# Rows of a tile in the order (chunk, step): new layouts for x, the parked rows and the states, and half the semaphore clears on ScalarE

## The chip, the cores and the metric

The kernel runs on one core of one Trainium2 chip. The metric is device time in microseconds (us) of one launch, the median of several runs.

## The reference, cut to what matters

Two blocks, each adding to x (8 batches, 1024 steps, 256 features, float32). The modulation vectors sa, ca, ga, sb, cb, gb come from a small matrix product with the condition vectors; ga and gb are kept away from zero.

```python
h = layernorm(x) * (1 + ca) + sa
# block 1: a recurrence over the 1024 steps of each batch
hs[t] = tanh(hs[t-1] @ A.T + h[:, t] @ B.T);  y[t] = hs[t] @ C.T
x = x + ga * (layernorm(y + h) * gamma + beta)
h = layernorm(x) * (1 + cb) + sb
# block 2: a recurrence over the 8 batches, each step on all 1024 rows
f = sigmoid(h[b] @ wf.T + c @ uf.T + bf); i = ...; g = tanh(...)
c = f * c + i * g
# after the last batch
x = x + gb * tanh(h @ wo.T + c_final @ uo.T + bo)
```

The scan of block 2 runs over the first axis, so its state c has one row for each position of the sequence. The kernel runs this scan for four blocks of positions, one after the other.

## The kernel before, in words

**Chunks.** Each batch is cut into K = 16 chunks of L = 64 steps. All 8 x 16 = 128 chunks are stepped together, so one step of block 1 is four products of 128 columns (two halves H of the features in, two out; the trace shows each as two PE instructions, since they are float32), and a state is 128 features x 128 chunks, twice. A first run over steps 18 to 63 of every chunk gives the state that the next chunk starts from; a check at the end (`again`) would repeat everything if a chunk's end state had moved since. In the profiled run there is one pass.

**Phase one** (`unit1`, to about 137 us) takes pairs of steps: SyncE (`SP`) loads 128 x 512 of x, VectorE (`DVE`), ScalarE (`ACT`) and GpSimd (`POOL`) normalise it, SP writes the normalised rows to a scratch tensor in HBM, `h_park` (L493), TensorE (`PE`) transposes them (L1425) and multiplies by B (L1408). Beside it the recurrence of the warm-up steps runs (`recur1`, L1373, then `summed`, L1448), with `tanhs`, `starts` and `summed` of ACT writing the states `hs` (L763, L768, L825).

**Phase two** (`unit2`) is a software pipeline, one tile after the other. There are 32 tiles; one is 256 rows, those of one batch and 16 steps of all its 16 chunks, in two halves j of 8 steps. The order on each engine is that of the calls in its own `unit2`. A unit holds: two steps of the recurrence (PE `step` L1462, DVE L1108 or L1111, ACT L832 or L835); `high` on ACT (L842) and `low` on POOL (L653, in phase one on DVE, L1095), which split the float32 states of a pair of steps into a rounded part `hsh` and a rest `hsl`; `project` (L1489), the product of these with C; the loads of the parked rows (`load_h`, L511) and of x (`load_x`, L518); normalisation, the three gates (L1503), the product with wo (L1557); and the store of a finished tile (`store`, L553), two DMAs of 128 x 256. Four states are held in `hs` (step t in slot t % 4), 8 steps in each half of `hsh` and `hsl`.

**The order of rows.** A tile's 128 partitions are in the order (step, chunk): 8 steps, and 16 chunks in each. `x_t`, `h_park_t` and `out_t` are the views that give this order for the three kinds of DMA.

**The end.** After the last unit, `last_outputs` on each engine finishes seven tiles that wait for the final c, and then the last tile in two halves (DVE L1283, POOL L728). SP reads the flag `again`, clears the first 25 of the 50 semaphores of `of_middle`, issues 14 stores in the order of `STORES` and the last two (L611), clears the other 25, waits until the four compute engines are through (`r_over`), clears the 20 of `of_end`, waits for all stores to land (`s_out`) and ends the round. `walk` and `rounds` only repeat the units.

Of the kernel before, what the change touches and what calls it, by code (L numbers as in the profile page):

```python
# [20 lines left out]
def adaln_kernel(nc, x, A, B, C, gamma, beta, wf, uf, bf, wi, ui, bi, wc, uc, bc, wo, uo, bo, in_c, cond, wmod, out):  # L21
# [71 lines left out]
    with ctx:  # L93
# [277 lines left out]
        def pair_of(t, first):  # L371

            return t[:, :, :, first:first + 2, :].rearrange("p m b t k -> p m b (t k)")

        def by_chunk(t):
            return t.rearrange("p (b k) -> p b k", b=NB)

        def by_half(t):
            return t.rearrange("p (m b k) -> p m b k", m=H, b=NB)
# [34 lines left out]
        def split_of(n, few, state_of):  # L414

            if n < NU - 2:
                return few[:, n % 2, :, :]
            i = (n - NU + 2) * H * POS
            return state_of[:, 0].rearrange("p m b t k -> p (m b t k)")[:, i:i + H * POS].rearrange("p (k n) -> p k n", k=H)
# [33 lines left out]
        def _(sp):  # L453
# [31 lines left out]
            def unit1(v, ref):  # L485
# [20 lines left out]
            def load_h(c):  # L506
# [3 lines left out]
                for i in range(2):  # L510
                    sp.dma_start(hin[:, c % 3, i * D:(i + 1) * D],  # L511
                                 h_park_t[b + i, T * TB + j * HT:T * TB + (j + 1) * HT, :, :]).then_inc(s_h[c % 3], 16)
# [32 lines left out]
            def store(o):  # L545
# [6 lines left out]
                for j in range(2):  # L552
                    sp.dma_start(out_t[o % NB, steps(o, j), :, :],  # L553
# [33 lines left out]
            with sp.Fori(0, left) as r:  # L587
# [17 lines left out]
                half = len(of_middle) // 2  # L605
                clear(of_middle[0:half])
                for o in STORES:
                    store(o)
                for j, done, n in ((0, s_fin, LAST + len(ON_DVE) + 1), (1, s_fp, len(ON_POOL) + 1)):
                    sp.wait_ge(done, n)  # L610
                    sp.dma_start(out_t[(NU - 1) % NB, steps(NU - 1, j), :, :], tiles_of(NU - 1)[:, j, :]).then_inc(s_out, 16)  # L611
                clear(of_middle[half:])
# [9 lines left out]
        def _(pool):  # L622
# [25 lines left out]
            def low(p):  # L648
# [4 lines left out]
                pool.tensor_tensor(pair_of(hsl[:, j], t), pair_of(hs, 2 * p % 4), pair_of(hsh[:, j], t).bitcast(f32),  # L653
# [1056 lines left out]
```

## Time and profile before

| what | value |
|---|---|
| median of 3 runs | 567.81 us (567.32 to 568.59) |
| the profiled execution's own time | 568.92 us |
| its span, first to last instruction | 567.0 us |
| PE busy | 546.8 us (96%) |
| DVE, ACT, POOL busy | 381.7, 341.6, 342.3 us |
| granted PE clock | 0.994 of full speed (2.4 GHz) |
| DMA | 64.09 MB in 58,513 packets, 49,736 of them under 2 KB |

PE is matrix multiplication; its weight loads (PEld) overlap it. Busy times of different engines lie beside each other, so a time counts towards the end only where the others wait for it. "Chain" is the line of work followed back from the last instruction, each piece to what released it. DMA instructions stand under SPq, the queue of SyncE that issues them; semaphore clears do not appear in the rows and show as gaps.

### The profile page before, as it was taken

The page shows a single profiled execution, that of the slowest core. Times are in us where ns is not written, and L with a number is a line of the kernel's source. Part 1 is how long each engine was busy: PE and PEld are TensorE (multiplying, and loading weights), DVE is VectorE, ACT ScalarE, POOL GpSimd, SP SyncE. Part 2 cuts the span into 40 slices and gives each one's busy share as a digit, 9 for nine tenths or more (in the row PEclk, how much of TensorE's full clock was granted, in tenths as well). Part 3 has the DMA queues.
Part 4 walks back from the last instruction along what each step waited for, and adds up shares of the span by engine and source line. Part 5 has one row for each costly group of instructions (what it writes and reads, how often), then busy time and mean ns, then how long its engine had stood idle before and what let it go on. Part 6 is the DMA issues. An engine that isn't in the chain of part 4 may idle for free.

```text
span 567.0 us, 13418 instructions
## 1 busy us (share of the span) xinstructions
PE 546.8 (96%) x4616; PEld 534.8 (94%) x4616; DVE 381.7 (67%) x908; ACT 341.6 (60%) x862; POOL 342.3 (60%) x475
## 2 busy tenths in 40 slices
PE   6999999999989999999999999999999999999992
PEld 3899999999879999999999999999999999999992
DVE  5888888885757665555766566666566677666763
ACT  3777777775466555465656565666655557567550
POOL 4677777660475444454766666677666667677353
PEclk9999999999999999999999999999999999999997
DMA  8556445435243222222233333333233343242354
GB/s 278 154 191 199 150 149 150 135 96 156 89 129 110 66 65 69 78 70 76 58 103 102 103 103 93 115 109 119 94 94 94 94 127 115 76 117 71 82 96 149
DMA packets 58513, 64.09 MB, mean 113 GB/s; under 512 B 5408, under 2 KB 49736, under 8 KB 58448
## 3 DMA queue, kind: packets, MB, share of 16 engines
q1 hardware_dynamic: 58448, 63.26, 37.1%
q8 instruction: 36, 0.59, 0.4%
q14 instruction: 29, 0.24, 0.1%
HBM read 46.44 MB, written 16.81 MB: 112 GB/s over the span
## 4 chain that ended last, share of the span: by engine, by line
PE 90%; DVE 3%; ACT 2%; POOL 2%; issue 1%; DMA 1%; SPq 0%; POOLq 0%; DVEq 0%; ACTq 0%
PE psOF L1503 14%; PE psI L1503 14%; PE psG L1503 13%; PE psWR L1557 7%; PE psWR L1462 7%; PE psWR L1408 4%; PE psOF L1408 4%; PE psWR L1373 4%; PE psC L1489 4%; PE psOF L1489 3%; PE psOF L1373 3%; PE psT L1536 2%; PE psT L1425 1%; PE psWR L1448 1%; PE psOF L1448 1%
## 5 line engine op out<-in xcount | busy, mean ns | idle before, releaser
L646 POOL TENSOR_TENSOR hin<-hin,uvec 128x256 f32<-128x256 f32 x64 | 51.0, 817 | 32.5 <-ACT hin L808 31.6
L653 POOL TENSOR_TENSOR hsl<-hs,hsh 128x512 fp32r<-128x512 f32 x24 | 30.9, 1288 | 51.5 <-DVE state L1215 31.6
L928 ACT ACTIVATE psOF<-psOF,biasT 128x256 f32<-128x256 f32 x64 | 26.0, 444 | 57.8 <-PE psOF L1503 57.8
L1203 DVE SCALAR_TENSOR_TENSOR lo<-psT,cb1T,hi 128x256 fp32r<-128x256 f32 x60 | 26.3, 480 | 46.5 <-ACT hi L873 46.5
L1111 DVE TENSOR_TENSOR pre<-psWR,state 128x256 f32<-128x256 f32 x44 | 18.6, 424 | 48.6 <-PE psWR L1462 48.6
L1462 PE MATMUL psWR<-hs,AT 128*128 128x128 f32 x368 | 49.6, 275 | 1.5 <-ACT hs L835 0.8
L660 POOL TENSOR_TENSOR xin<-xin,tA 128x512 f32<-128x512 f32 x32 | 41.5, 1298 | 12.7 <-DMA tA<-rows_d 12.7
L687 POOL TENSOR_TENSOR zn<-zn,tA 128x512 f32<-128x512 f32 x32 | 41.3, 1292 | 12.4 <-ACT zn L846 12.4
L846 ACT ACTIVATE zn<-state,nmA,rstdA 128x256 f32<-128x256 f32 x64 | 35.0, 594 | 20.3 <-POOL nmA L677 20.3
L1462 PEld LDWEIGHTS psWR<-hs,AT 128*128 128x128 f32 x368 | 45.3, 191 | 1.9 <-ACT hs L835 1.0
L1065 DVE SCALAR_TENSOR_TENSOR hin<-xin,mvA,uvec 128x256 f32<-128x256 f32 x56 | 40.3, 759 | 9.8 <-DMA h_park<-hin 9.4
L682 POOL TENSOR_TENSOR wx<-wx,tG 128x512 f32<-128x512 f32 x24 | 36.5, 1519 | 11.2 <-ACT wx L894 11.1
L700 POOL TENSOR_TENSOR wx<-wx,uvec 128x512 f32<-128x512 f32 x24 | 31.1, 1295 | 14.6 <-DVE state L1215 12.5
L846 ACT ACTIVATE xn<-state,nmB,rstdB 128x256 f32<-128x256 f32 x64 | 34.8, 590 | 5.6 <-POOL nmB L709 5.6
L928 ACT ACTIVATE gg<-psG,biasT 128x256 f32<-128x256 f32 x64 | 27.0, 475 | 16.6 <-PE psG L1503 16.6
L835 ACT ACTIVATE hs<-pre 128x256 f32<-128x256 f32 x44 | 18.4, 417 | 30.4 <-DVE pre L1111 30.2
L1503 PE MATMUL psOF<-hi,wfT_hi 128*128 128x256 f32 x120 | 33.6, 280 | 2.4 <-DVE gf L1223 2.4
L1503 PE MATMUL psI<-hi,wiT_hi 128*128 128x256 f32 x120 | 35.9, 299 | 0.0
L928 ACT ACTIVATE psI<-psI,biasT 128x256 f32<-128x256 f32 x64 | 26.0, 446 | 14.9 <-PE psI L1503 14.9
L808 ACT ACTIVATE hin<-hin,rstdA 128x256 f32<-128x256 f32 x64 | 28.7, 497 | 9.6 <-POOL rstdA L639 9.6
L1503 PE MATMUL psOF<-lo,wfT_hi 128*128 128x256 f32 x120 | 33.3, 278 | 0.0
L1503 PE MATMUL psI<-lo,wiT_hi 128*128 128x256 f32 x120 | 33.3, 278 | 0.0
(351 smaller groups left out, 2306.5 us busy)
## 6 DMA issues: line engine op xcount, KB each, us to landing
h_park<-hin SPq DMA_DIRECT2D x32, 256.0 KB, 2.2
hin<-h_park SPq DMA_DIRECT2D x64, 128.0 KB
xin<-in_L_attn_x_dram SPq DMA_DIRECT2D x64, 128.0 KB
tA<-rows_d SPq DMA_DIRECT2D x32, 256.0 KB, 4.4
out_dram<-state SPq DMA_DIRECT2D x64, 128.0 KB
xin<-in_L_attn_x_dram SPq DMA_DIRECT2D x28, 256.0 KB, 2.9
tW<-rows_d SPq DMA_DIRECT2D x32, 128.0 KB, 3.9
tG<-rows_d SPq DMA_DIRECT2D x24, 128.0 KB, 4.1
```

Source lines behind the costliest of these rows:

```text
L646: pool.tensor_tensor(h, h, sa, ALU.add).then_inc(a_h, 1)
L660: pool.tensor_tensor(xg, xg, both(tA[:, m % 2, D:W]), ALU.add).then_inc(s_xg, 1)
L687: pool.tensor_tensor(two(zn[:, :]), two(zn[:, :]), both(tA[:, m % 2, 0:D]), ALU.mult).then_inc(s_zg, 1)
L846: act.activation(dst[:, j * D:(j + 1) * D], tiles_of(m)[:, j, :], ACT.Identity, bias=nm[:, j:j + 1], scale=rstd[:, j:j + 1]).then_inc(done, 1)
L928: act.activation(dst[:, m_ * POS:(m_ + 1) * POS], src[:, m_ * POS:(m_ + 1) * POS], fn, bias=biasT[:, i, m_, n % NB:n % NB + 1]).then_inc(s, 1)
L1065: dve.scalar_tensor_tensor(halfw(dst, tt), halfw(src, tt), mv[:, tt, 0:1], ca1, ALU.subtract, ALU.mult).then_inc(a_tmp, 1)
L1373: ins = pe.matmul(sums1(v.c - R1LAG)[m][:, tt * P:(tt + 1) * P], AT[:, k, m * P:(m + 1) * P], hs[:, k, :, 1 - tt, :], start=False, stop=(k ...
L1408: last = pe.matmul(ps, w["B"][:, k, m * P:(m + 1) * P], h[:, (ref - back) % 2, k * 2 * P:(k + 1) * 2 * P], start=(n % (3 * H) == 0), stop= ...
L1462: ins = pe.matmul(ps, AT[:, k, m * P:(m + 1) * P], hs[:, k, :, (t - 1) % 4, :], start=(k == 0 and (separate or m == 0)), stop=(k == H - 1 ...
L1489: last = pe.matmul(ps[:, i * D:(i + 1) * D], h[:, j, k, b + i, :, :].rearrange("p t k -> p (t k)"), w["C"][:, k, :], start=(n == 1 and i = ...
L1503: last = pe.matmul(ps[:, at + m * columns:at + (m + 1) * columns], w[name][:, k, m * P:(m + 1) * P], xx[:, k, :], start=(start and n == 1) ...
L1557: last = pe.matmul(ps[:, j * D:(j + 1) * D], h[:, k, j * P:(j + 1) * P], w["wo"][:, k, :], start=(n < HELD and c == 1 and j == 0), stop=(c ...
```

## The change: what it does

1. DRAM side: rows of a tile go in the order (chunk, step); `x_t`, `out_t` are rearranged, `h_park` is laid out as [chunk row, step, feature], like x.
2. `hs` becomes [slot, half, chunk row], so a state is one contiguous run. `hsh` and `hsl` get the step as innermost axis: for one chunk row its 8 steps lie side by side. So `high` and `low` now read `hs` in runs of 128 and read or write `hsh`, `hsl` at a stride of 8 elements (32 bytes), where before all runs had 32 elements.
3. The clears of the first half of `of_middle` move from SP, where they stood ahead of the stores, to the end of ACT.

```diff
-    x_t = x.rearrange("b (k t) d -> b t k d", k=K)
-    out_t = out.rearrange("b (k t) d -> b t k d", k=K)
+    x_t = x.rearrange("b (k t) d -> b k t d", k=K)
+    out_t = out.rearrange("b (k t) d -> b k t d", k=K)
-    h_park = nc.dram_tensor("h_park", [L, P, D], f32, kind="Internal").ap()
-    h_park_t = h_park.rearrange("t (b k) d -> b t k d", b=NB)
+    h_park = nc.dram_tensor("h_park", [P, L, D], f32, kind="Internal").ap()
...
-        hsh = sb("hsh", [P, 2, H, NB, HT, K], f32r)
-        hsl = sb("hsl", [P, 2, H, NB, HT, K], f32r)
-        hs = sb("hs", [P, H, NB, 4, K])
+        hsh = sb("hsh", [P, 2, H, P, HT], f32r)
+        hsl = sb("hsl", [P, 2, H, P, HT], f32r)
+        hs = sb("hs", [P, 4, H, P])
...
         def pair_of(t, first):
-            return t[:, :, :, first:first + 2, :].rearrange("p m b t k -> p m b (t k)")
+            return t[:, :, :, first:first + 2].rearrange("p m n t -> p m t n")
+
+        def two_of(first):
+            return hs[:, first:first + 2, :, :].rearrange("p t m n -> p m t n")
+
+        def step_of(t):
+            return hs[:, t, :, :].rearrange("p m n -> p (m n)")
...
-                    sp.dma_start(h_park[bass.ds(p * 2, 2), :, :].rearrange("t p d -> p t d"),
+                    sp.dma_start(h_park[:, bass.ds(p * 2, 2), :],
                                  two(htok(ref - 2)))...
...
                     sp.dma_start(hin[:, c % 3, i * D:(i + 1) * D],
-                                 h_park_t[b + i, T * TB + j * HT:T * TB + (j + 1) * HT, :, :])...
+                                 h_park[(b + i) * K:(b + i + 1) * K, T * TB + j * HT:T * TB + (j + 1) * HT, :])...
...
-                                 x_t[m % NB, steps(m, j), :, :]).then_inc(s_x[m % 2], 16)
+                                 x_t[m % NB, :, steps(m, j), :]).then_inc(s_x[m % 2], 16)
...
-                    sp.dma_start(out_t[o % NB, steps(o, j), :, :],
+                    sp.dma_start(out_t[o % NB, :, steps(o, j), :],
...
                 sp.wait_ge(s_Ul, 2)
-                half = len(of_middle) // 2
-                clear(of_middle[0:half])
                 for o in STORES:
                     store(o)
...
-                clear(of_middle[half:])
+                clear(of_middle[len(of_middle) // 2:])
...
-                pool.tensor_tensor(pair_of(hsl[:, j], t), pair_of(hs, 2 * p % 4), pair_of(hsh[:, j], t).bitcast(f32),
+                pool.tensor_tensor(pair_of(hsl[:, j], t), two_of(2 * p % 4), pair_of(hsh[:, j], t).bitcast(f32),
                                    ALU.subtract).then_inc(s_hsl, 1)
...
-                    act.activation(hs[:, :, :, t % 4, :], by_half(pre[:, :]), ACT.Tanh).then_inc(s_tanh, H)
+                    act.activation(step_of(t % 4), pre[:, :], ACT.Tanh).then_inc(s_tanh, H)
...
-                act.activation(pair_of(hsh[:, j], t), pair_of(hs, 2 * p % 4), ACT.Copy).then_inc(s_hsh, 1)
+                act.activation(pair_of(hsh[:, j], t), two_of(2 * p % 4), ACT.Copy).then_inc(s_hsh, 1)
...
                 act.activation(psR[:, 0:D], psR[:, 0:D], ACT.Tanh).then_inc(s_ot, 1)
+                act.wait_ge(s_fin, LAST + 1)
+                for s in of_middle[0:len(of_middle) // 2]:
+                    act.sem_clear(s)
...
                         ins = pe.matmul(sums1(v.c - R1LAG)[m][:, tt * P:(tt + 1) * P], AT[:, k, m * P:(m + 1) * P],
-                                        hs[:, k, :, 1 - tt, :], start=False, stop=(k == H - 1), skip_group_check=True)
+                                        hs[:, 1 - tt, k, :], start=False, stop=(k == H - 1), skip_group_check=True)
...
-                            last = pe.matmul(ps[:, i * D:(i + 1) * D], h[:, j, k, b + i, :, :].rearrange("p t k -> p (t k)"), w["C"][:, k, :],
+                            last = pe.matmul(ps[:, i * D:(i + 1) * D], h[:, j, k, (b + i) * K:(b + i + 1) * K, :].rearrange("p k t -> p (k t)"), w["C"][:, k, :],
```

The other edits write the same forms at the other places that touch `hs` (the tanhs of phase one, `starts`, the copies `h_end` and `h_skip`, the check at the end, the products L1448 and L1462).

## Rows read from the trace of the kernel before

**Rows 1.** Busy us (instructions) of PE, PEld, DVE, ACT, POOL; PEclk; DMA share; GB/s.

```profile
0.00:17.00 17.00, 11.96 (x33) 5.62 (x34) 10.88 (x32) 6.17 (x13) 8.35 (x23) 1.00 0.78 263
137.00:170.00 33.00, 29.77 (x254) 27.68 (x252) 22.19 (x67) 15.79 (x43) 17.37 (x26) 1.00 0.40 123
170.00:444.00 274.00, 273.96 (x2367) 273.57 (x2367) 173.48 (x411) 160.54 (x390) 165.24 (x217) 1.00 0.30 90
```

**Rows 2.** State products and transposes (L1536): ns min/median/max, first and last start.

```profile
L1462 PE MATMUL psWR<-hs,AT x368: 270/275/377, 142.8 to 435.8; 128*128 128x128 f32 x184
...
L1536 PE MATMUL psT<-ident,xn x128: 270/272/328, 153.4 to 530.0; 128*128 128x128 f32 x128
```

**Rows 3.** Groups by shape: high, low, two state copies: us busy, mean ns.

```profile
L653 POOL TENSOR_TENSOR hsl<-hs,hsh 128x512 fp32r<-128x512 f32 x24 | 30.9, 1288 | 51.5 <-DVE state L1215 31.6 <-DVE state L1147 19.9
...
L842 ACT ACTIVATE hsh<-hs 128x512 fp32r<-128x512 f32 x32 | 20.1, 628 | 0.3
...
L1095 DVE TENSOR_TENSOR hsl<-hs,hsh 128x512 fp32r<-128x512 f32 x8 | 5.5, 682 | 1.7 <-ACT hsh L842 1.7
...
L1191 DVE COPY h_skip<-hs 128x256 f32<-128x256 f32 x1 | 0.6, 640 | 0.0
...
L1101 DVE COPY h_end<-hs 128x256 f32<-128x256 f32 x1 | 0.3, 294 | 0.1
```

**Rows 4.** ACT in phase one: start us, us, instruction, idle before it.

```profile
115.50 0.67 ACT L825 ACTIVATE hs<-psOF 128x128 f32<-128x128 f32 x2 [0.72 <-PE psOF L1448]
```

**Rows 5.** ACT and POOL at the start of phase two, in order of time.

```profile
153.24 0.61 ACT L842 ACTIVATE hsh<-hs 128x512 fp32r<-128x512 f32 x1
...
154.14 1.27 POOL L653 TENSOR_TENSOR hsl<-hs,hsh 128x512 fp32r<-128x512 f32 x1
155.37 0.24 POOL L677 TENSOR_TENSOR nmA<-ngA,rstdA 128x2 f32<-128x2 f32 x1
```

**Rows 6.** The chain in the same stretch: start us, us, what.

```profile
156.03 1.10 ACT zn L846 x2
...
159.30 1.28 POOL hsl L653
...
170.04 1.60 PE psOF L1503 x12
```

**Rows 7.** Waits over the span: waiting instruction, releaser: us, times, longest.

```profile
ACT psOF L928 <- PE psOF L1503: 57.8, 28, 2.9
...
POOL nmB L709 <- ACT ngB L862: 36.0, 25, 2.8
...
SPq L500 <- DMA out_dram<-state: 0.6, 1, 0.6
```

**Rows 8.** DMA instructions on SP by line: ns min/median/max.

```profile
L493 SPq DMA_DIRECT2D h_park<-hin x32: 373/384/410, 11.0 to 126.5; - x32
...
L553 SPq DMA_DIRECT2D out_dram<-state x62: 593/642/707, 282.2 to 561.2; - x62
```

**Rows 9.** SP about its clears and at the end: start us, us.

```profile
282.19 1.34 SPq L553 DMA_DIRECT2D out_dram<-state  x2
287.90 0.67 SPq L511 DMA_DIRECT2D hin<-h_park  x1
...
548.08 1.25 SPq L553 DMA_DIRECT2D out_dram<-state  x2
...
552.56 1.37 SPq L553 DMA_DIRECT2D out_dram<-state  x2
...
561.95 1.34 SPq L611 DMA_DIRECT2D out_dram<-state  x2
```

**Rows 10.** The first and the last of the results stored at the end.

```profile
550.53 0.69 DVE L1278 TENSOR_TENSOR state<-psI,state 128x512 f32<-128x512 f32 x1
...
558.05 0.72 POOL L728 TENSOR_TENSOR state<-wx,state 128x256 f32<-128x256 f32 x1
```

**Rows 11.** A window after the last computation, columns as in rows 1.

```profile
561.00:566.00 5.00, 0.00 (x0) 0.00 (x0) 0.00 (x0) 0.00 (x0) 0.00 (x0) 0.50 0.53 186
```

More of the change, by code:

```diff
@@ L418, in split_of @@
             i = (n - NU + 2) * H * POS
-            return state_of[:, 0].rearrange("p m b t k -> p (m b t k)")[:, i:i + H * POS].rearrange("p (k n) -> p k n", k=H)
+            return state_of[:, 0].rearrange("p m n t -> p (m n t)")[:, i:i + H * POS].rearrange("p (k n) -> p k n", k=H)
         def hi_at(n):
@@ L610, in _ @@
                     sp.wait_ge(done, n)
-                    sp.dma_start(out_t[(NU - 1) % NB, steps(NU - 1, j), :, :], tiles_of(NU - 1)[:, j, :]).then_inc(s_out, 16)
-                clear(of_middle[half:])
+                    sp.dma_start(out_t[(NU - 1) % NB, :, steps(NU - 1, j), :], tiles_of(NU - 1)[:, j, :]).then_inc(s_out, 16)
+                clear(of_middle[len(of_middle) // 2:])
                 sp.wait_ge(r_over, r * 4 + 4)
@@ L762, in tanhs @@
                     act.wait_ge(a_r, v.lin(4, -4 * R1LAG + 2 * tt + m + 1))
-                    act.activation(hs[:, m, :, tt, :], by_chunk(sums1(v.c - R1LAG)[m][:, tt * P:(tt + 1) * P]), ACT.Tanh).then_inc(a_tanh, 1)
+                    act.activation(hs[:, tt, m, :], sums1(v.c - R1LAG)[m][:, tt * P:(tt + 1) * P], ACT.Tanh).then_inc(a_tanh, 1)
             def starts():
                 for m in range(H):
-                    act.activation(hs[:, m, :, 3, 1:K], by_chunk(sums1(RP1 - 1)[m][:, P:2 * P])[:, :, 0:K - 1], ACT.Tanh).then_inc(a_start, 1)
+                    act.activation(by_chunk(hs[:, 3, m, :])[:, :, 1:K], by_chunk(sums1(RP1 - 1)[m][:, P:2 * P])[:, :, 0:K - 1], ACT.Tanh).then_inc(a_start, 1)
             def unit1(v, ref):
@@ L824, in summed @@
                     act.wait_ge(s_r, 2 * t + m + 1)
-                    act.activation(hs[:, m, :, t % 4, :], by_chunk(sums1(RP1 + t // 2)[m][:, t % 2 * P:(t % 2 + 1) * P]), ACT.Tanh).then_inc(s_tanh, 1)
+                    act.activation(hs[:, t % 4, m, :], sums1(RP1 + t // 2)[m][:, t % 2 * P:(t % 2 + 1) * P], ACT.Tanh).then_inc(s_tanh, 1)
             def step(t):
@@ L831, in step @@
                         act.wait_ge(s_pre, n_pre(t) + m + 1)
-                        act.activation(hs[:, m, :, t % 4, :], by_chunk(pre[:, m * P:(m + 1) * P]), ACT.Tanh).then_inc(s_tanh, 1)
+                        act.activation(hs[:, t % 4, m, :], pre[:, m * P:(m + 1) * P], ACT.Tanh).then_inc(s_tanh, 1)
                 else:
                     act.wait_ge(s_pre, n_pre(t) + 2)
-                    act.activation(hs[:, :, :, t % 4, :], by_half(pre[:, :]), ACT.Tanh).then_inc(s_tanh, H)
+                    act.activation(step_of(t % 4), pre[:, :], ACT.Tanh).then_inc(s_tanh, H)
             def high(p):
@@ L1094, in low @@
                 j, t = p // 4 % 2, p % 4 * 2
-                dve.tensor_tensor(pair_of(hsl[:, j], t), pair_of(hs, 2 * p % 4), pair_of(hsh[:, j], t).bitcast(f32),
+                dve.tensor_tensor(pair_of(hsl[:, j], t), two_of(2 * p % 4), pair_of(hsh[:, j], t).bitcast(f32),
                                   ALU.subtract).then_inc(s_hsl, 1)
@@ L1100, in boundary @@
                 dve.wait_ge(a_tanh, 4 * RP1)
-                dve.tensor_copy(by_half(h_end[:, :]), hs[:, :, :, 1, :]).then_inc(a_end, 1)
+                dve.tensor_copy(h_end[:, :], step_of(1)).then_inc(a_end, 1)
             def step(t):
@@ L1190, in unit2 @@
                     dve.wait_ge(s_tanh, 4 * SP0)
-                    dve.tensor_copy(by_half(h_skip[:, :]), hs[:, :, :, (SKIP - 1) % 4, :]).then_inc(s_skip, 1)
+                    dve.tensor_copy(h_skip[:, :], step_of((SKIP - 1) % 4)).then_inc(s_skip, 1)
                 if u == ML:
@@ L1238, in unit2 @@
                     dve.wait_ge(s_hsl, PAIRS)
-                    dve.tensor_tensor(by_half(pre[:, :]), hs[:, :, :, (L - 1) % 4, :], by_half(h_end[:, :]), ALU.subtract).then_inc(k_diff, 1)
+                    dve.tensor_tensor(pre[:, :], step_of((L - 1) % 4), h_end[:, :], ALU.subtract).then_inc(k_diff, 1)
                     dve.wait_ge(k_diff, 1)
-                    near = hs[:, 0, 0:4, :, :].rearrange("p b t k -> p (b t k)")
+                    near = step_of(0)
                     dve.tensor_scalar(near, pre[:, :], -TOL, None, ALU.is_ge).then_inc(k_diff, 1)
@@ L1286, in body @@
                 prepare()
-                dve.tensor_copy(hs[:, :, :, 1, :], by_half(h_skip[:, :])).then_inc(a_end, 1)
-                dve.memset(hs[:, :, :, 3, 0:1], 0.0).then_inc(a_end, 1)
+                dve.tensor_copy(step_of(1), h_skip[:, :]).then_inc(a_end, 1)
+                dve.memset(by_chunk(step_of(3))[:, :, 0:1], 0.0).then_inc(a_end, 1)
                 walk(dve, RUNS1, unit1)
@@ L1448, in summed @@
                         ins = pe.matmul(sums1(RP1 + t // 2)[m][:, t % 2 * P:(t % 2 + 1) * P], AT[:, k, m * P:(m + 1) * P],
-                                        hs[:, k, :, (t - 1) % 4, :], start=False, stop=(k == H - 1), skip_group_check=True)
+                                        hs[:, (t - 1) % 4, k, :], start=False, stop=(k == H - 1), skip_group_check=True)
                     ins.then_inc(s_r, 1)
```

8 lines of the change are left out of this document (3 added, 5 removed).

## Prediction

> **What bounds the kernel now.** I read the page's busy shares, then the busy time by stretches, then PE's waits, and then the end of the span alone. PE is busy 96% of the span and holds 90% of the chain. From 170 to 444 us it is busy 273.96 of 274.00 us [rows 1]: the reader is to see that nothing a feeding engine gains there can count, and that it loses nothing either while its slack lasts. Three places differ. One is the length of PE's own instructions. The second is the start of phase two, 137 to 170 us, where PE is idle 3.2 us [rows 1] and the chain leaves it for POOL, ACT and DVE until 170.04 [rows 6]. The third is the end: the last result is done at 558.05 + 0.72 = 558.77 us [rows 10], the span ends at 567.0, and all 8.2 us between belong to SP and the stores. Of the profiled execution's 568.92 us, 1.9 lie outside the span. It ran 1.11 us above the median of the runs, 567.81; I make the sum on the profile and take the difference off the median.
>
> **The stores at the end.** SP issues 16 DMAs from 552.56 to 561.95 + 1.34 = 563.29 us, 0.671 us each [rows 9]. They form a queue with no gap: the last result is 3.2 us old when its store begins. While they drain and no engine computes, the DMA share is 0.53 at 186 GB/s, 8.5 of 16 engines [rows 11]. So the pattern (8 steps outside, 16 chunks inside) uses eight engines, and these are full. Loads with 128 rows outside reach 0.78, 12.5 engines, in the first 17 us [rows 1]; after the change 16 chunks are outside, and I assume that more than eight work, up to 16. At 16 x 128 KB = 2.1 MB and 186 GB/s the stores need 11.3 us; issue alone needs nearly the same 10.7.
> The Trainium skill, DMA: Bandwidth & Descriptors, "Why a DMA increments its semaphore by 16 and not by 1", says that the number of engines is the largest up to 16 that divides the outermost dimension on both sides: 8 before, 16 after the change. The trace agrees (8.5 engines here).
>
> The clears: 69 of them stood between 282.19 + 1.34 and 287.90 us, 4.37 us, so 0.063 us each [rows 9]. Before the 16 stores SP is free at 549.33 and starts at 552.56 [rows 9]; this gap holds the flag's load and 25 clears (1.6 us). The first result was ready at 550.53 + 0.69 = 551.22 [rows 10]. Without the clears the load ends at about 552.56 - 1.6 = 551.0, so the first store starts at 551.27: 1.3 us earlier. On ACT the 25 clears come after its last tanh, beside DVE's and POOL's last work and the stores; they cost nothing unless ACT ends later than SP's queue, which leaves them some 3 us.
>
> How long one issue takes is the first open number. A tile's store takes 0.593 to 0.707 us, 0.642 at the median; the store of parked rows, with 256 runs of 1 KB instead of 128, only 0.384 [rows 8]. So the count of runs does not set it; either the eight engines or the different shapes of the two sides do. Only the first goes away. Bounds: 0.384 + 0.05 between issues = 0.43 us, and 0.65 (0.593 + 0.05, with the queue less loaded). I take 0.65, the instruction's own row, since the shapes still differ. Then issues end at 551.27 + 16 x 0.65 = 561.7 instead of 563.3. Behind the last issue SP has 45 clears, 2.84 us, and before it waited another 0.6 for the last landing [rows 7]. With the engines half loaded a store lands beside the clears, so the end follows 3.1 instead of 3.7 us after the issues: 564.8 us, **2.2 us less**. At 0.43 us the queue follows the results instead: the last two issues start at 558.4 and 558.85, end at 559.3, and the span ends at 562.4, 4.6 less.
>
> **PE.** The products with the states read 128 columns in 8 runs of 16; they take 275 ns at the median, a transpose that reads 128 columns in one run 272 [rows 2]. Six groups (L1373, L1448, L1462) hold 880 such instructions, the largest of them is shown. At 3 ns each that is 2.6 us; if the runs are not the reason it is 0. The 48 between 137 and 170 us, where PE waits anyway, don't count. I take **2.0 us less**, a little under the row, since the medians are whole ns.
>
> **High and low.** Before: ACT 628 ns, DVE 682, POOL 1288 [rows 3]. After, each element written goes 32 bytes on, and so do those read from `hsh`. No row shows such an access. Lower bound: no loss, since runs of 16 and 32 elements cost none. Upper bound: the slowest copy of a state took 640 ns where the same shape took 294 [rows 3] (POOL was in `low` beside it), a factor of 2.2, so 1370, 1490 and 2810 ns. I take 1.5, in the middle: 0.31 us more on ACT, 0.34 on DVE, 0.64 on POOL.
> The Trainium skill bears on this twice. Vector Engine (DVE) Microarchitecture Reference, "Measured stream behaviour on trn2", has full rate only for runs of two adjacent words and 2.5 instead of 1.05 ns a column for a step of 24 words; GPSIMD Engine Reference, "Performance pitfalls for Q7 kernels", has half as much again for reads with a step over 8 bytes. No row here shows either. The second gives my value for POOL; the first would be a factor of 2.4, and its sum is the rival below.
>
> Where it counts: in full flow not at all. ACT waits 2.1 us a unit for PE ahead of the first gate, which comes after `high`, and POOL waits 1.4 us a unit for ngB, which comes after `low` [rows 7]. In phase one ACT has 0.72 us idle a unit [rows 4], so `high` may grow by that. At the start of phase two it does count. ACT's `high` (153.24) precedes the mean that POOL needs for nmA (155.37), POOL's `low` (154.14) stands right before it [rows 5], and the next `low` (159.30) is itself a piece of the chain that ends with PE's restart at 170.04 [rows 6]. With ACT longer by d and POOL by p the restart is later by d + 2p less about 0.3 of slack (ACT began the normalisation behind it at 156.03 [rows 6], nmA was there at 155.61). 0.31 + 1.28 - 0.3 = **1.3 us more**; the ends are 0 and 0.74 + 3.04 - 0.3 = 3.5. If the cover in full flow were gone, each of 22 units would add the excess.
>
> **The rest.** Parked rows are written as 128 runs of 2 KB instead of 256 of 1 KB, tile loads spread over more engines: no chain piece waits for them, cost 0. Tanhs write one run instead of 8 or 16: below 0.03 us each, on engines with slack, 0. The copies and the check: single instructions, 0.
>
> **Sum.** -2.2 - 2.0 + 1.3 = -2.9 us: profile 566.0, median **564.9 us**.
>
> **Rivals.**
> A: the eight engines were what made an issue slow. For it: rows with sixteen engines are at 0.384. Against: those have equal shapes on both sides. 2.4 us more gain: 562.5. Chance 0.22.
> B, the other side: the strided access is expensive. It acts at the three pieces at 153, 154 and 159 us, and from a factor of 2.1 also on ACT in phase one, where the idle 0.72 is used up and PE waits in each of about four units. With factor f the price is 3.2(f - 1) - 0.3; it outweighs the 4.2 us of gains from f = 2.4, and with phase one from 2.3. At f = 3: 6.1 at the restart, 4 x 0.5 in phase one, less 4.2: 571.7. For it: one access per line of memory everywhere in `high` and `low`. Against: these engines already take 2.5 ns (POOL) and 1.2 ns (ACT) an element, which may cover it. Chance 0.13. At the skill's factor of 2.4 on all three the sum would be about 568.3, the mildest form of B.
> C: the 3 ns on PE have another cause (a product is not a transpose) and stay: 566.9, within the noise. Chance 0.15; a store that still uses eight engines would look the same in the total, with the queue as full as before.
> Forecast: 0.50, with its own range 563.4 to 566.3.
>
> **How the numbers follow.** Best of all bounds: -4.6 - 2.6 = 560.6. Worst short of B: -2.2 + 3.5 = 569.1. The range for 8 in 10 goes from 562.2, just under A, through the forecast and C to 567.8, leaving most of B and the coincidence of all gains outside. This kernel's runs tell 0.2% (1.1 us) from no change. Faster: the forecast and A, 0.72; same: C, 0.15; slower: B, 0.13.
>
> **What would show it.** Stores: the DMA share at the end no longer flat at 0.53, the first store 0.1 us behind its result instead of 1.3, the last issue to the end about 3.1 us. Issue: the median of L553, 0.6 or 0.4. PE: the median of L1373, L1448 and L1462 at 272. Strides: mean of L842, L653, L1095 near 0.94, 1.93 and 1.02 us, and PE's restart in phase two about 1.3 us later against its own start. Wrong would be a PE that shows waits in full flow, or a store queue as long as before.

## Result: 0.4% slower, and the profile after

| | before | after |
|---|---|---|
| median of 6 runs each, us | 568.20 (567.32 to 568.98) | 570.46 (569.39 to 572.00) |
| ratio to before, 95% interval | | 1.0041 [1.0026, 1.0056] |
| profiled execution, us | 568.92 | 571.36 |
| its span, us | 567.04 | 569.48 |
| last result done, us | 558.77 | 562.30 |
| from there to the end, us | 8.3 | 7.2 |

I had forecast 564.9, in a range of 562.2 to 567.8. The kernel became slower. The end got shorter by 1.1 us, TensorE's own instructions did not change, and the last result came 3.5 us later.

The end of phase one before, then two stretches of the kernel after, columns as in [rows 1]:

```profile
105.00:137.00 32.00, 32.00 (x284) 32.00 (x282) 23.18 (x50) 24.26 (x68) 14.59 (x22) 1.00 0.37 115
```

```profile
105.00:137.00 32.00, 31.35 (x268) 30.56 (x267) 25.87 (x49) 26.23 (x64) 16.99 (x22) 1.00 0.36 113
170.00:444.00 274.00, 272.73 (x2357) 272.13 (x2356) 174.50 (x414) 173.67 (x393) 170.38 (x216) 1.00 0.31 90
```

The stretch from 105 to 137 us is the one to see. TensorE was busy for all 32.00 us of it before; now 0.65 us is missing, in the last units of phase one, which my sum did not contain. The last row looks like a loss in full flow and is none: it begins at 170 us, and the restart is now at 173.85.

State products and transposes after, against [rows 2] (ns min/median/max):

```profile
L1466 PE MATMUL psWR<-hs,AT x368: 270/275/377, 146.1 to 439.6; 128*128 128x128 f32 x184
...
L1540 PE MATMUL psT<-ident,xn x128: 270/273/329, 156.7 to 533.8; 128*128 128x128 f32 x128
```

The product still takes 275 ns, although its 128 columns now lie in one run. The gap to a transpose is not the layout.

`high` and `low` by shape, against [rows 3]:

```profile
L654 POOL TENSOR_TENSOR hsl<-hs,hsh 128x512 fp32r<-128x512 f32 x24 | 38.9, 1620 | 51.6 <-DVE state L1219 31.4 <-DVE state L1151 19.9 <-ACT ngA L858 0.3
L843 ACT ACTIVATE hsh<-hs 128x512 fp32r<-128x512 f32 x32 | 37.9, 1184 | 0.3
...
L1099 DVE TENSOR_TENSOR hsl<-hs,hsh 128x512 fp32r<-128x512 f32 x8 | 9.1, 1133 | 1.5 <-ACT hsh L843 1.5
```

They grew by factors of 1.89 (ACT), 1.66 (DVE) and 1.26 (POOL). I had taken 1.5 for all three.

### Where the 3.5 us come from

Three places: phase one, its end, and the restart in phase two. The first two were not in my sum, and both have VectorE's `low` in them. First, VectorE in phase one. Its timeline after (start us, us, instruction):

```profile
112.21 1.11 DVE L1099 TENSOR_TENSOR hsl<-hs,hsh 128x512 fp32r<-128x512 f32 x1
113.22 0.69 DVE L1081 TENSOR_TENSOR lo<-psT,hi 128x512 fp32r<-128x512 f32 x1
...
114.75 0.25 DVE L1056 BATCH_NORM_AGGREGATE mvA<-stA 128x2 f32<-128x6 f32 x2 [0.18 <-DVE stA L1044]
115.07 0.48 DVE L1069 SCALAR_TENSOR_TENSOR hin<-xin,mvA,uvec 128x256 f32<-128x256 f32 x1
115.48 0.95 DVE L1069 SCALAR_TENSOR_TENSOR hin<-xin,mvA,uvec 128x256 f32<-128x256 f32 x1
116.35 1.10 DVE L1099 TENSOR_TENSOR hsl<-hs,hsh 128x512 fp32r<-128x512 f32 x1
```

and the same unit before:

```profile
112.04 0.68 DVE L1095 TENSOR_TENSOR hsl<-hs,hsh 128x512 fp32r<-128x512 f32 x1
112.64 0.68 DVE L1077 TENSOR_TENSOR lo<-psT,hi 128x512 fp32r<-128x512 f32 x1
...
114.48 0.88 DVE L1065 SCALAR_TENSOR_TENSOR hin<-xin,mvA,uvec 128x256 f32<-128x256 f32 x1
115.28 0.47 DVE L1065 SCALAR_TENSOR_TENSOR hin<-xin,mvA,uvec 128x256 f32<-128x256 f32 x1
115.68 0.68 DVE L1095 TENSOR_TENSOR hsl<-hs,hsh 128x512 fp32r<-128x512 f32 x1
```

From one `low` to the next it was 3.64 us, TensorE's own pace, now it is 4.14. 0.43 of the 0.50 us are `low`, 0.07 the two scalar_tensor_tensor. In both kernels the rows name no wait of VectorE in the unit but the 0.18 us between its own statistics and their aggregate. That does not make it full: one of the two scalar_tensor_tensor takes 0.88 or 0.95 us, the other 0.47. The long one overlaps an addition of GpSimd to `hin` and ends 0.28 us behind it. This holds for each of the 627 scalar_tensor_tensor of phase one that took over 0.53 us in the 14 traces (0.27 to 0.30 us). In the kernel after this is the addition:

```profile
115.20 0.95 POOL L647 TENSOR_TENSOR hin<-hin,uvec 128x256 f32<-128x256 f32 x1
```

So 0.4 to 0.5 us of each unit was waiting that stands in the rows as work.

TensorE needs `lo`, which stands behind `low`, and it and its weight loads now wait for it (waiting instruction, releaser: us, times, longest; 107 to 137 us):

```profile
PE psWR L1412 <- DVE lo L1081: 0.3, 1, 0.3
PE psOF L1412 <- DVE lo L1081: 0.2, 1, 0.2
```

```profile
PEld psOF L1412 <- DVE lo L1081: 0.8, 2, 0.4
PEld psWR L1412 <- DVE lo L1081: 0.5, 1, 0.5
PEld psOF L1452 <- ACT hs L826: 0.2, 1, 0.2
```

Matmul by matmul, about 1.5 of the 1.76 us that TensorE falls back in phase one (table below) are lost at three such waits for `lo`, and 0.25 at one wait for ScalarE's `hs`.

Second, the end of phase one. VectorE after, from 137 us:

```profile
139.72 1.30 DVE L1099 TENSOR_TENSOR hsl<-hs,hsh 128x512 fp32r<-128x512 f32 x1 [1.50 <-ACT hsh L843]
140.91 0.18 DVE L993 COPY c0z<-c 128x2 f32<-128x2 f32 x1
...
142.36 0.18 DVE L1000 TENSOR_TENSOR c0z_lo<-c0z,c0z_hi 128x16 fp32r<-128x16 f32 x1
```

and TensorE, which waits for the last of these, and its restart in phase two:

```profile
142.68 0.28 PE L1583 MATMUL psG<-woT_hi,sbT_hi 128*8 128x256 f32 x1 [1.36 <-DVE c0z_lo L1000]
...
173.85 0.36 PE L1507 MATMUL psOF<-hi,wfT_hi 128*128 128x256 f32 x1 [1.27 <-DVE gf L1227]
```

The last `high` (1.28 us) and the last `low` (1.30) stand in series here, and the small tables of `split_tables()` behind them. Before, the pair took 0.63 + 0.69 us and TensorE did not wait.

The program's matmuls are the same 4616 in every kernel here, in one order, so the start of a given one can be compared with its start before. The first 17 us differ between executions (in these traces from 1.3 us shorter to 0.5 us longer than in the kernel before), so the table takes off the shift at 16 us. In the measured times this spread remains: the 98 runs of the kernel before beside the experiments go from 567.00 to 570.39 us. The three columns are the matmuls that start at 137, 142 and 200 us in the kernel before:

| kernel | 137 | 142 | 200 |
|---|---|---|---|
| after | 1.76 | 3.30 | 3.80 |
| clearsback (after, clears on SyncE again) | 1.75 | 3.20 | 3.69 |
| locont (`hsl` whole runs) | 1.75 | 3.35 | 3.84 |
| hicont (`hsh` whole runs) | 0.42 | 1.20 | 1.28 |
| lowfree (`low` cheap, `high` dear) | 0.22 | 1.18 | 1.20 |
| contall (both whole runs) | 0.03 | 0.03 | 0.02 |
| lowafter (`low` behind `lo`) | 0.01 | 1.52 | 2.01 |
| lowtab (and tables ahead of the last `low`) | 0.01 | 0.01 | 0.50 |
| pairs | 0.02 | 0.02 | 0.66 |
| mixed | 0.01 | 0.01 | 0.27 |
| b_park (before, parked rows alone) | -0.02 | -0.02 | 0.00 |
| b_clears (before, clears alone) | 0.01 | 0.01 | 0.00 |
| b_clears_2 (the same kernel) | 0.01 | 0.01 | -0.01 |

After: 1.76 in phase one, 1.54 at its end, 0.50 at the restart.

### The profile page after: what moved, and what is told of

Same layout as the page of the kernel before. It is cut to its first block, busy times and chain, and to the rows that moved or that the text cites. A ratio compares the mean times of both kernels' runs of the same rounds, so it can differ in the third digit from the quotient of the medians.

```text
span 569.5 us, 13419 instructions
## 1 busy us (share of the span) xinstructions
PE 546.6 (96%) x4616; PEld 534.4 (94%) x4616; DVE 389.9 (68%) x908; ACT 358.7 (63%) x862; POOL 352.4 (62%) x475
## 4 chain that ended last, share of the span: by engine, by line
PE 82%; POOL 4%; issue 4%; DVE 3%; ACT 2%; DMA 2%; SPq 1%; POOLq 0%; DVEq 0%; ACTq 0%
PE psOF L1507 14%; PE psI L1507 13%; PE psG L1507 13%; PE psWR L1561 7%; PE psWR L1466 6%; PE psWR L1377 4%; PE psOF L1377 3%; PE psWR L1412 3%; PE psOF L1412 3%; PE psC L1493 3%; PE psOF L1493 3%; PE psT L1540 2%; PE psT L1429 1%; PE psC L1429 1%; PE psOF L1570 1%
## 5 line engine op out<-in xcount | busy, mean ns | idle before, releaser
L654 POOL TENSOR_TENSOR hsl<-hs,hsh 128x512 fp32r<-128x512 f32 x24 | 38.9, 1620 | 51.6 <-DVE state L1219 31.4
L1069 DVE SCALAR_TENSOR_TENSOR hin<-xin,mvA,uvec 128x256 f32<-128x256 f32 x56 | 43.9, 823 | 7.3 <-DMA h_park<-hin 5.7
L843 ACT ACTIVATE hsh<-hs 128x512 fp32r<-128x512 f32 x32 | 37.9, 1184 | 0.3
L809 ACT ACTIVATE hin<-hin,rstdA 128x256 f32<-128x256 f32 x64 | 28.7, 497 | 10.4 <-POOL rstdA L640 10.2
```

Source lines behind the costliest of these rows:

```text
L654: pool.tensor_tensor(pair_of(hsl[:, j], t), two_of(2 * p % 4), pair_of(hsh[:, j], t).bitcast(f32), ALU.subtract).then_inc(s_hsl, 1)
L843: act.activation(pair_of(hsh[:, j], t), two_of(2 * p % 4), ACT.Copy).then_inc(s_hsh, 1)
L1069: dve.scalar_tensor_tensor(halfw(dst, tt), halfw(src, tt), mv[:, tt, 0:1], ca1, ALU.subtract, ALU.mult).then_inc(a_tmp, 1)
```

## Experiments

Theory 1: the element-strided `high` and `low` cost the 3.5 us, through VectorE in phase one. Rival 2: it is ScalarE's `high` that delays phase one. Theory 3: it is the parked rows' new transfers. Medians are of 11 or 12 runs (6 for clearsback), against 29 to 35 runs of the kernel before on the same chip. The shifts in the table are of one profiled execution each.

### contall, hicont, locont, lowfree: which strided operand

```diff
-        hsh = sb("hsh", [P, 2, H, P, HT], f32r)
+        hsh = sb("hsh", [P, 2, H, HT, P], f32r)   # contall, hicont
-        hsl = sb("hsl", [P, 2, H, P, HT], f32r)
+        hsl = sb("hsl", [P, 2, H, HT, P], f32r)   # contall, locont, lowfree
...
-   tensor_tensor(pair_of(hsl[:, j], t), two_of(2 * p % 4), pair_of(hsh[:, j], t).bitcast(f32),
+   tensor_tensor(pair_of(hsl[:, j], t), two_of(2 * p % 4), two_of(2 * p % 4),   # lowfree
...
```

`pair_of` and `project` follow the layout and are left out here. In all four, `project` takes its columns as they lie, so the rows of a tile are misplaced in the changed operand; lowfree also leaves the low part of the states out of the result. The instructions and their sizes stay.

**contall.** 

> The changed kernel with hsh and hsl laid out as [P, 2, H, HT, P], so that high() and low() read and write whole runs of 128 elements; project() takes its 128 columns flat, so rows of a projected tile belong to one step of 128 chunks instead of 16 chunks by 8 steps: the values are misplaced, the amount of work on each engine is the same. Theory 1 (the element-strided high and low cost the +3.5 us, by way of VectorE in phase one): high back near 630 ns, low on VectorE near 680 ns, on GpSimd near 1290 ns, the shift of the last result (562.30) back to 558.8 to 559.1, total 567.0 to 567.6 against 568.2 before, so 0.1 to 0.25 per cent faster. Theory 3 (the new layout of the parked rows and their transfers delays phase one): the time stays near 570.5.

Measured: 567.68 us, ratio 0.9985 [0.9973, 0.9997]. All three places of the loss are at 0.03 us or less. The strides are the whole loss; theory 3 falls. The clears and the new rows are still in this kernel, and it is 0.15% faster than before.

**hicont.** 

> The changed kernel with hsh alone as [P, 2, H, HT, P] (high() writes whole runs, low() reads whole runs of it and still writes hsl with the step innermost); project() takes hsh's columns flat, so the values are misplaced. Theory 1 (VectorE is the one without slack in phase one, low stands ahead of lo on it): high falls to about 630 ns and low on VectorE from 1107 to 850 to 1000 ns (one of its two strided operands is left), so a part, 1 to 2.5 us, of the 3.5 us comes back: 568 to 569.5. Rival 2 (it is ScalarE's high, +0.56 us a unit, that delays phase one): nearly all comes back, 567.0 to 567.6.

Measured: 568.43 us, 1.0001 [0.9990, 1.0013]. **locont.** 

> The changed kernel with hsl alone as [P, 2, H, HT, P] (low() writes whole runs of it and reads hsh with the step innermost; high() writes with the step innermost as in the changed kernel); project() takes hsl's columns flat, so the values are misplaced. Theory 1: high stays near 1180 ns, low on VectorE falls to 700 to 950 ns, 1 to 2.5 us come back (568 to 569.5), more than in the kernel with hsh alone made contiguous if the write costs more than the read. Rival 2 (ScalarE's high delays phase one): nothing comes back, 570.3 to 570.6.

Measured: 571.13 us, 1.0044 [1.0030, 1.0058]. The groups of hicont (first) and locont:

```profile
L655 POOL TENSOR_TENSOR hsl<-hs,hsh 128x512 fp32r<-128x512 f32 x24 | 31.2, 1302 | 51.5 <-DVE state L1220 31.6 <-DVE state L1152 19.9
L844 ACT ACTIVATE hsh<-hs 128x512 fp32r<-128x512 f32 x32 | 20.1, 628 | 0.3
L1100 DVE TENSOR_TENSOR hsl<-hs,hsh 128x512 fp32r<-128x512 f32 x8 | 8.9, 1115 | 1.3 <-ACT hsh L844 1.3
```

```profile
L655 POOL TENSOR_TENSOR hsl<-hs,hsh 128x512 fp32r<-128x512 f32 x24 | 38.3, 1594 | 51.7 <-DVE state L1220 31.4 <-DVE state L1152 19.9 <-ACT ngA L859 0.3
...
L1100 DVE TENSOR_TENSOR hsl<-hs,hsh 128x512 fp32r<-128x512 f32 x8 | 8.9, 1110 | 1.5 <-ACT hsh L844 1.5
```

I had expected half of VectorE's cost from each of its two strided operands. It is not so: one strided operand, read or written, costs as much as two (1115, 1110, 1133 ns). On GpSimd only the read costs (1594); the strided write is nearly free (1302 against 1288). So locont could not return anything, and its time says nothing for rival 2, as I had written it would. But hicont does speak against theory 1 as it stood: VectorE's `low` is as slow there as in the kernel after, and phase one loses only 0.42 us.

**lowfree.** 

> The changed kernel in which high() still writes hsh with the step innermost, while low() reads hs twice in place of hs and hsh (so it computes zeros) and writes whole runs into hsl; project() takes hsl's columns flat. The low part of the states is left out of the result; waits, counts and sizes are the same. With the two kernels before it this is the fourth of four: both cheap 567.68, low alone dear 568.43, both dear 570.46 to 571.1. Theory 1b (the two costs are not additive: the period of 4.14 us in phase one needs GpSimd's rstdA to be held back by VectorE's long low, and high only shifts it under that low; at the end of phase one high and low stand in series): high near 1180 ns, low near 680 ns, rstdA back to 0.8 us, no wait of TensorE for lo, at the end of phase one 0.5 to 0.7 us more than the kernel with both cheap: 568.0 to 568.5. Rival 2 (high alone delays phase one, low costs no more than 0.75): 569.8 to 570.5, with TensorE waiting for lo as in the changed kernel.

Measured: 568.21 us, 1.0003 [0.9993, 1.0013]; `high` 1185 ns, `low` on VectorE 682. Rival 2 falls too: the dear `high` alone costs 0.22 us in phase one. At the end of phase one it costs 0.96, more than the 0.5 to 0.7 that I expected, and `rstdA` took 1.03 us there, not 0.8. "Dear" is the strided form, "cheap" the one in whole runs. Between lowfree and the kernel after, both with the dear `high`, the dear `low` makes 1.54 us of phase one (0.22, then 1.76).

**What the four do not show.** Phase one loses 0.03 us with neither dear, 0.42 with `low` alone, 0.22 with `high` alone, 1.76 with both. It looks as if the costs were not additive, but hicont was profiled in another order of two small events than the other three. These are `low` on VectorE and the power `rstdA` on GpSimd, in the kernel before, in hicont, in contall and in the kernel after:

```profile
115.49 0.82 POOL L639 TENSOR_TENSOR rstdA<-veA,mhalf 128x2 f32<-128x2 f32 x1
115.68 0.68 DVE L1095 TENSOR_TENSOR hsl<-hs,hsh 128x512 fp32r<-128x512 f32 x1
```

```profile
114.21 0.82 POOL L641 TENSOR_TENSOR rstdA<-veA,mhalf 128x2 f32<-128x2 f32 x1
114.39 1.09 DVE L1100 TENSOR_TENSOR hsl<-hs,hsh 128x512 fp32r<-128x512 f32 x1
```

```profile
115.57 0.68 DVE L1100 TENSOR_TENSOR hsl<-hs,hsh 128x512 fp32r<-128x512 f32 x1
115.78 1.03 POOL L641 TENSOR_TENSOR rstdA<-veA,mhalf 128x2 f32<-128x2 f32 x1
```

```profile
116.35 1.10 DVE L1099 TENSOR_TENSOR hsl<-hs,hsh 128x512 fp32r<-128x512 f32 x1
116.56 1.46 POOL L640 TENSOR_TENSOR rstdA<-veA,mhalf 128x2 f32<-128x2 f32 x1
```

Where `rstdA` starts ahead of `low`, it takes 0.82 us, however long `low` is. Where it starts behind, it ends 0.56 us behind the end of `low`, so 1.03 us with a cheap `low` and 1.46 with a dear one. Nine traces are of the second kind (0.55 to 0.57 us), strided or not. Three are of the first: before, b_clears and hicont. (In lowafter and lowtab, below, `low` was moved.) One kernel can be in either, as b_clears and b_clears_2 are. In those three the landing of the parked rows, which releases VectorE at the start of these units, came at 110.7 to 110.9 us; in the five traces of the second kind with a cheaper `high`, at 110.4 to 110.6 (the start-up taken off). With the dear `high`, GpSimd's additions come 0.35 us later (110.38 in place of 110.03), and the order was the second one also with a late landing (clearsback, 110.77). So the dear `high` does bring the order about that costs, but a cheap one does not exclude it, and what hicont would lose in it no trace shows. Its twelve runs, 568.43 at the median, lie 2.0 us under the kernel after.

In the kernel after this closes a circle:

```profile
113.91 0.91 ACT L809 ACTIVATE hin<-hin,rstdA 128x256 f32<-128x256 f32 x2 [0.17 <-POOL rstdA L640]
...
114.50 1.65 POOL L647 TENSOR_TENSOR hin<-hin,uvec 128x256 f32<-128x256 f32 x2 [0.62 <-ACT hin L809]
```

`low` ends at 113.32, `rstdA` 0.56 us behind it, ScalarE waits for it and scales `hin`, GpSimd waits for that and adds, up to 116.14. VectorE's scalar_tensor_tensor ends 0.28 us behind the addition, and the next `low` ends at 117.45: 4.13 us, the unit. In hicont, lowfree and the kernel before ScalarE has no wait for `rstdA` in these units, and VectorE gives back what its `low` takes: in hicont one unit is 3.64 us, with 0.96 us for the two scalar_tensor_tensor in place of 1.35, and the next 3.97. So theory 1b, which holds the 4.14 us to need the late `rstdA`, fits the rows. That VectorE is held up by GpSimd's addition, and GpSimd by `low`, I infer from the constant distances; no semaphore says it.

### lowafter and lowtab: the order on VectorE

```diff
-                if ahead and p > 0:
-                    low(p - 1)
                 ...
                     dve.tensor_tensor(hmT_lo[:, b, :], ...)      # lo
+                if ahead and p > 0:
+                    low(p - 1)                                   # lowafter, lowtab
...
+                split_tables()                                   # lowtab; was in unit2
                 low(AP - 1)
```

> The changed kernel with one move: in phase one VectorE's low(p - 1) stands behind the low half of the transposed tile (hmT_lo) instead of ahead of it; nothing else is changed. Theory 1 in its narrow form (TensorE waits for hmT_lo, which stands behind the longer low): 1 to 2 us come back, but VectorE's sum a unit, 4.1 us, stays over TensorE's 3.65, so not all: 568.5 to 569.7. Rival 2 (ScalarE's high delays phase one) and theory 3 (the parked rows' transfers): no change, 570.3 to 570.6.

Measured: 569.22 us, 1.0018 [1.0005, 1.0032]. VectorE:

```profile
112.64 0.68 DVE L1079 TENSOR_TENSOR lo<-psT,hi 128x512 fp32r<-128x512 f32 x1
113.25 1.23 DVE L1099 TENSOR_TENSOR hsl<-hs,hsh 128x512 fp32r<-128x512 f32 x1
...
115.61 1.03 DVE L1069 SCALAR_TENSOR_TENSOR hin<-xin,mvA,uvec 128x256 f32<-128x256 f32 x2
116.56 0.68 DVE L1079 TENSOR_TENSOR lo<-psC,hi 128x512 fp32r<-128x512 f32 x1
117.16 1.28 DVE L1099 TENSOR_TENSOR hsl<-hs,hsh 128x512 fp32r<-128x512 f32 x1
```

The 1.76 us in phase one are gone, with `high` and `low` as long as ever. The unit takes 3.91 us, and `lo` comes ahead of the long instruction. `rstdA` starts ahead of `low` here and takes 0.82 us, and ScalarE does not wait for it: the circle is open. How much the open circle and the earlier `lo` give was not separated. The second place stays (1.51 us), so I moved the tables:

> The changed kernel with low(p - 1) behind the low half of the transposed tile in phase one, as in the run before, and split_tables() moved out of phase two's first unit to ahead of the last low of phase one. TensorE's wait of 1.3 to 1.4 us at shift_wo for c0z_lo should go, since the tables no longer stand behind high(7) and low(7) in series. If that series is the second place of the loss: 569.2 less 1.3 to 1.9, so 567.4 to 567.9, faster than before by 0.1 to 0.2 per cent. If the projection of the first tile needs that high and low as well, or the restart takes what is saved: 568.7 to 569.2.

Measured: 568.09 us, 0.9993 [0.9982, 1.0004]. TensorE's wait is gone:

```profile
136.79 0.18 DVE L1000 TENSOR_TENSOR c0z_lo<-c0z,c0z_hi 128x16 fp32r<-128x16 f32 x1
137.99 1.31 DVE L1099 TENSOR_TENSOR hsl<-hs,hsh 128x512 fp32r<-128x512 f32 x1 [1.01 <-ACT hsh L843]
```

Two moves on VectorE take back 3.3 of the 3.8 us without touching the layout. The median, though, is a little above what I expected (567.4 to 567.9).

### pairs and mixed: the order of the elements

```diff
-            return t[:, :, :, first:first + 2].rearrange("p m n t -> p m t n")
+            return t[:, :, :, first:first + 2]
-            return hs[:, first:first + 2, :, :].rearrange("p t m n -> p m t n")
+            return hs[:, first:first + 2, :, :].rearrange("p t m n -> p m n t")
```

(mixed: GpSimd's `low` keeps the order of the kernel after; its lines are left out here.)

> The changed kernel, but high() and low() walk their operands in the order (chunk, step) and not (step, chunk): hsh and hsl are then written and read in pairs of adjacent words, hs is read with a step of 1 KB between the two words of a pair. If what makes high and low slow is that each word is alone in its 32 bytes: high 630 to 900 ns, low 680 to 900 ns, 568 to 569.3. If the hopping read of hs costs as much as the lone writes: high near 1180, low near 1100, 570.3 to 570.8. It cannot be told beforehand from any row; the first is taken with 0.5.

Measured: 568.45 us, 1.0001 [0.9991, 1.0010]. The groups:

```profile
L654 POOL TENSOR_TENSOR hsl<-hs,hsh 128x512 fp32r<-128x512 f32 x24 | 44.5, 1854 | 51.2 <-DVE state L1219 31.3 <-DVE state L1151 19.9
L843 ACT ACTIVATE hsh<-hs 128x512 fp32r<-128x512 f32 x32 | 24.2, 756 | 0.3
L1099 DVE TENSOR_TENSOR hsl<-hs,hsh 128x512 fp32r<-128x512 f32 x8 | 5.6, 701 | 1.7 <-ACT hsh L843 1.7
```

The same bytes in the same places: with the step innermost in the access as in the memory, VectorE is at 701 ns in place of 1133 and ScalarE at 756 in place of 1184. GpSimd becomes slower (1854 against 1620), so it kept the old order in the next one.

> The changed kernel with high() on ScalarE and low() on VectorE in the order (chunk, step), as in the kernel with pairs, and low() on GpSimd in the changed kernel's order (step, chunk), which took 1.62 us there against 1.86 with pairs. The restart, 0.6 us late with pairs, should be 0.3 to 0.45 late: 568.1 to 568.3, against 568.45 with pairs; nothing in phase one.

Measured: 567.55 us, 0.9989 [0.9975, 1.0002], under the 568.1 to 568.3 that I expected; the restart is 0.27 late. The interval holds 1, so it is not shown to be faster than before. Pairs together with the two moves on VectorE were not run.

### b_park, b_clears and clearsback: the rest of the change

```diff
-            h_park = nc.dram_tensor("h_park", [L, P, D], f32, kind="Internal").ap()
+            h_park = nc.dram_tensor("h_park", [P, L, D], f32, kind="Internal").ap()    # b_park
...
-                half = len(of_middle) // 2
-                clear(of_middle[0:half])                                              # b_clears
...
+                act.wait_ge(s_fin, LAST + 1)
+                for s in of_middle[0:len(of_middle) // 2]:
+                    act.sem_clear(s)
```

(clearsback: the kernel after with the second edit undone.)

> The kernel before with the parked rows alone laid out as [P, L, D] (written in runs of 2 KB, read with a row of the tile 1 KB times L from the next); tiles, states, stores and clears stay as before. Theory 1b (none of the loss is in the parked rows): within 0.1 per cent of before, 568.0 to 568.5, and no shift of TensorE's matmuls between 112 and 137 us. Theory 3 (the parked rows' transfers delay phase one's last units): 1 to 3.5 us slower.

Measured: 568.19 us, 0.9996 [0.9984, 1.0009]. No shift anywhere; the parked rows cost nothing, as predicted.

> The kernel before with one edit: the first half of the semaphores of the middle is cleared by ScalarE at its end and no longer by SyncE ahead of the last stores. If the clears on SyncE are what the changed kernel's shorter tail comes from (1.0 us shorter from the last result to the end): 1.0 to 1.3 us faster, 567.1 to 567.4. If the gain of the tail comes from the stores' new row order (16 engines in place of 8): 568.2 to 568.5.

Measured: 567.48 us, 0.9995 [0.9985, 1.0006]. 

> The kernel before with the clears moved alone, once more beside these three, since its first runs gave a median 0.75 us under the kernel before's but a ratio of 0.9995 with 1 inside the interval. If the 1.0 us of the tail is real it is 567.1 to 567.6 and the ratio 0.9980 to 0.9990; if the launches' own spread made it, 568.0 to 568.4.

Measured: 566.57 us, 0.9974 [0.9965, 0.9984]. The two results of the one kernel lie further apart than their intervals allow, on two chips; both medians are below the kernel before's, and by both traces the way from the last matmul's start to the end of the span is shorter (9.88 and 9.75 us against 10.67). The first, just above my 567.1 to 567.4, has 1 in its interval, the second is better than the 567.1 that I expected at best. How large the gain is between 0.05 and 0.26% stays open; by the second result it is the best kernel of this study.

> The changed kernel with the first half of the middle's clears back on SyncE ahead of the last stores, as before the change; the rows, layouts and transfers stay changed. With the run that moved the clears alone this makes two by two. In the traces so far the time from the last result to the end falls by about 1.0 us with the clears alone and by about 1.0 with the whole change, in which the fourth of the last stores takes 1.4 to 1.8 us to issue in place of 0.6. If the new rows alone bring nothing to the tail (the slow fourth issue eats what they bring): 1.0 to 1.3 us above the changed kernel, 571.5 to 571.8, ratio to before 1.0055 to 1.0062. If the rows bring the gain of the tail and the clears are hidden beside it: 570.4 to 570.8. The page also shows whether the fourth issue is slow without the moved clears.

Measured: 571.20 us, 1.0054 [1.0036, 1.0073], between my two ranges. From the last matmul's start to the end it takes 10.30 us, the kernel after 9.58. So of the tail's 1.1 us the clears give 0.7 to 0.9 and the new rows 0.2 to 0.4. The second is little more than the noise of one trace: b_park, whose tail is that of the kernel before, takes 10.94 us for 10.67.

SP's stores in the kernel after:

```profile
554.83 0.56 SPq L556 DMA_DIRECT2D out_dram<-state  x1
...
556.82 1.41 SPq L556 DMA_DIRECT2D out_dram<-state  x1
...
565.05 1.20 SPq L612 DMA_DIRECT2D out_dram<-state  x2
```

The first starts 0.1 us behind its result (554.75). The fourth takes 1.41 us; the median of the line is 0.600. All ten kernels with the new rows have one such issue: the fourth takes 1.41 to 2.10 us in six, the fifth 0.94 to 1.24 in three (lowafter, locont, mixed), the second 1.20 in clearsback. In the four traces with the old rows the slowest of the 16 takes 0.66 to 0.90. From the end of the last issue to the end of the span it takes 3.21 to 3.26 us with the new rows and 3.76 to 4.07 with the old. What the slow issue waits for I don't know.

## Why the prediction was wrong, step by step

**High and low in phase one: the step that failed.** I wrote that "in phase one ACT has 0.72 us idle a unit [rows 4], so `high` may grow by that", and let the strided access count there only from a factor of 2.1, on ScalarE. ScalarE's growth of 0.56 us did fit in its 0.72, and alone it cost 0.22 us. But VectorE also does a `low` in each of these units. I had not looked at its timeline in phase one, so I priced its 0.34 us at nothing. With the dear `high` in place the dear `low` cost 1.54 us more: the unit went from TensorE's 3.64 to 4.14 us, and `lo` came late for TensorE. By the rows it goes through GpSimd's `rstdA`, which ends behind `low`; that route is inferred, the 1.76 us are measured. The last `high` and `low` of the phase, in series ahead of the tables, cost another 1.54. Together 3.3 us, where I had 0.

**The factor.** 1.5 was low for ScalarE (1.89) and VectorE (1.66) and high for GpSimd (1.26). Rival B needed 2.3 to outweigh the gains; no engine reached it, and the kernel was slower all the same, by a place that B had not in it. The Trainium skill, Vector Engine (DVE) Microarchitecture Reference, "Measured stream behaviour on trn2", whose rule I had weighed, gives full rate for pairs of adjacent words; the trace agrees (701 ns with pairs, 682 with whole runs). Its factor of 2.4 is for a longer step than this one and is not borne out here (1.66). GPSIMD Engine Reference, "Performance pitfalls for Q7 kernels", has half as much again for strided reads; here it is 1.24, and the measurement decides.

**The restart.** Predicted +1.3 us from d + 2p - 0.3. With the measured 0.56 and 0.33 this gives 0.9; the traces show 0.50. By contall, where it is 0, the strides are the cause, as forecast, but the size was 2.6 times too large, and with the measured lengths still nearly double. In the trace of lowtab the 0.50 us are there before the restart, at TensorE's waits for ScalarE's `hs` (at 161.5 us by the clock of the kernel before) and `xn` (at 163.1).

**TensorE.** Predicted -2.0, measured 0: 275 ns as before, and no shift between 200 and 440 us. Rival C was right. A difference between a product and a transpose is no measure of a layout.

**The stores.** Predicted -2.2, measured -1.1 (8.3 to 7.2). The start behind the result (0.1 us), the issue (0.600, 0.64 with its gap) and the way from the last issue to the end (3.23, predicted 3.1) were right. The DMA share at the end rose from 0.53 [rows 11] to 0.75, in the same window, which now begins 1.3 us ahead of the last result (0.71 from 562 to 567 us):

```profile
561.00:566.00 5.00, 0.00 (x0) 0.00 (x0) 0.86 (x2) 0.00 (x0) 1.23 (x2) 0.82 0.75 206
```

So more than eight engines work (0.75 x 16 = 12), but the queue of 16 stores took 11.4 us, longer than the 10.7 before: 554.83 to 566.25. I had forecast 10.4, and had named a queue as long as before as a sign of being wrong. The slow fourth issue takes 0.8 us of it. Rival A fell: with more than eight engines an issue takes 0.600 us in place of 0.642, not 0.384.

**The sum by its measured terms:** +1.76 + 1.54 + 0.50 - 1.1 = +2.7, and the span grew by 2.4; 0.3 us are made up between 440 us and the last result (shift 3.80, then 3.53).

## What to carry to other kernels

Before an instruction is made longer, read the timeline of every engine that runs it in every stage that it stands in, and ask of each whether its unit is as long as the bottleneck's. VectorE was busy only 23.2 of the 32 us from 105 to 137 before the change, and still had no idle time in the units in which `low` stood. Nor does a line without gaps say that an engine is full: 0.4 us and more of VectorE's unit was one instruction running long beside GpSimd's. And where two orders of events are possible, one trace a kernel is not enough to compare: look whether both were in the same one. A layout that makes one engine's access whole makes another's strided: the order in which both sides are walked is free, and pairs of adjacent words were almost as good as whole runs on VectorE and ScalarE. Price each edit of a bundle alone: the only gain here that needs no new layout was the clears.

## What the runs showed of the hardware

- A 128x512 ScalarE copy to every eighth float32 word takes 1184 ns against 628 in whole runs; in pairs of words, read from two places, 756.
- A 128x512 VectorE tensor_tensor takes 1110 to 1133 ns with one or with two strided operands, 682 with none, 701 in pairs (means of 8).
- The same on GpSimd: 1288 with none, 1302 with the write strided, 1594 with one read strided, 1620 with both, 1854 in pairs; 1042 when both reads are the same tile.
- GpSimd's 128x2 power that started 0.2 us behind a VectorE 128x512 tensor_tensor ended 0.55 to 0.57 us behind the end of that one, in nine traces, whether it took 0.68 or 1.10 us, with strided operands or without. Started 0.2 us ahead of it, the power took 0.82 us.
- A VectorE 128x256 scalar_tensor_tensor takes 0.47 us; those that took longer (up to 1.02) overlapped GpSimd's 128x256 addition and ended 0.28 us behind it.
- A store of 128 rows takes 0.600 us to issue in the new row order and 0.642 in the old; with the new order one of the last 16 took 0.94 to 2.10, in every kernel.
